# A transformer block on one core: the rounds of its pipeline in a hardware loop, and the input statistics one step later

## What is computed

```python
def _layernorm(x, axis=-1, eps=1e-05):
    m = jnp.mean(x, axis=axis, keepdims=True)
    v = jnp.var(x, axis=axis, keepdims=True)
    return (x - m) / jnp.sqrt(v + eps)

# ffn(x) = x @ int4(kernel) + bias + (x @ a) @ b      128 -> 128, rank 16
x = x + 0.5 * ffn(layernorm(x))
x = x + attn(layernorm(x))     # 16 heads of 64, latent of 32, causal softmax over 512 tokens
x = x + 0.5 * ffn(layernorm(x))

# attn: q = x Wq; latent = x Wkv_down; k = latent Wk_up; v = latent Wv_up
# y = softmax(mask(q k^T / 8)) v; out = y Wout
```

## Time and profile before

| | |
|---|---|
| median of 3 runs | 1116.89 us (1111.92 to 1118.87) |
| the profiled execution | 1111.92 us, its span 1110.2 us |
| mean granted clock of TensorE | 0.959 |
| PE matmul, busy | 995.7 us, 90% of the span, 7518 instructions |
| DVE, busy | 760.2 us, 68%, 2840 instructions |
| ACT, busy | 526.4 us, 47% |
| POOL, busy | 357.0 us, 32% |
| instruction queues | 116 packets, 1.44 MB |

### The profile page before, as it was taken

The page is one execution under the profiler, slowest core; times in us unless marked ns, Lnnn a source line. Parts: engine busy times, 40 slices in busy tenths (PEclk is TensorE's granted clock), DMA queues, the critical chain, the costliest instruction groups (busy, mean ns, idle before and its releaser), DMA issues. The chain is left out here.

```text
span 1110.2 us, 22533 instructions
## 1 busy us (share of the span) xinstructions
PE 995.7 (90%) x7518; PEld 592.3 (53%) x7518; DVE 760.2 (68%) x2840; ACT 526.4 (47%) x1089; POOL 357.0 (32%) x527
## 2 busy tenths in 40 slices
PE   5758899999999999999999999999999999999983
PEld 3434545555555465555555555655555555656453
DVE  2257577778677777778787877777786777776412
ACT  0110445555545545455545555455555455454550
POOL 1010213424243423424243424234242424232432
PEclk9965799999999999999999999999999999999996
DMA  3062323240423324231413333241404233230000
GB/s 73 10 142 58 87 59 96 49 99 21 108 54 68 96 59 106 59 97 25 108 43 77 87 68 96 59 106 43 99 25 105 59 69 87 58 87 2 21 20 10
DMA packets 72436, 74.81 MB, mean 67 GB/s; under 512 B 8880, under 2 KB 46016, under 8 KB 72320
## 3 DMA queue, kind: packets, MB, share of 16 engines
q1 hardware_dynamic: 72320, 73.37, 28.0%
HBM read 9.90 MB, written 8.39 MB: 16 GB/s over the span
## 5 line engine op out<-in xcount | busy, mean ns | idle before, releaser
L750 DVE CUSTOM_DVE_ANT_0 bank<-bank,corner 128x128 f32<-128x128 f32 (+3 forms) x1024 | 487.7, 509 | 223.1 <-PE bank L564 216.4
L405 ACT ACTIVATE probs<-bank 128x512 f32<-128x512 f32 (+1 forms) x704 | 373.9, 558 | 446.5 <-PE bank L517 444.8
L564 PE MATMUL bank<-keys,q_stack 96*128 96x128 f32 (+3 forms) x1024 | 321.6, 362 | 35.8 <-DVE maxima L750 15.9
L371 POOL TENSOR_SCALAR_AFFINE_SELECT probs<-probs 128x512 f32<-128x512 f32 x256 | 162.2, 634 | 573.0 <-ACT probs L405 572.9
L517 PE MATMUL bank<-q_stack,keys 97*128 97x512 f32 (+3 forms) x1024 | 328.2, 380 | 19.7 <-ACT probs L405 19.5
L564 PEld LDWEIGHTS bank<-keys,q_stack 96*128 96x128 f32 x1024 | 188.9, 197 | 166.1 <-issue 99.8
L517 PEld LDWEIGHTS bank<-q_stack,keys 97*128 97x128 f32 x1024 | 172.2, 191 | 109.4 <-ACT probs L405 77.4
L531 PE MATMUL bank<-probs,lat 128*32 128x512 f32 (+3 forms) x2048 | 192.1, 447 | 0.6 <-ACT y_sb L412 0.3
L542 PE MATMUL bank<-probs,group_ones 128*32 128x512 f32 (+3 forms) x2048 | 185.7, 434 | 1.9 <-ACT den L434 0.4
L750 DVE DVE_READ_ACCUMULATOR2_ANT maxima<- 128x1 f32 x1024 | 144.3, 141 | 0.5
L542 PEld LDWEIGHTS bank<-probs,group_ones 128*32 128x32 f32 x2048 | 64.1, 110 | 81.3 <-issue 54.7
(11 more groups left out here) (98 smaller groups left out, 615.4 us busy)
## 6 DMA issues: line engine op xcount, KB each, us to landing
q_stack<-q_high SPq DMA_DIRECT2D x256, 128.0 KB, 2.4
q_stack<-q_low SPq DMA_DIRECT2D x128, 128.0 KB, 2.5
out_dram<-x SPq DMA_DIRECT2D x32, 256.0 KB, 2.3
x_in<-in_L_attn_x_bld_dram SPq DMA_DIRECT2D x16, 256.0 KB, 3.3
x_back<-out_dram SPq DMA_DIRECT2D x16, 256.0 KB, 3.1
keys<-keys_staged SPq DMA_DIRECT2D x16, 192.0 KB, 2.5
lat<-lat_staged SPq DMA_DIRECT2D x16, 64.0 KB, 1.9
wq_in<-in_L_attn_Wq_dram SPq DMA_DIRECT2D x1, 512.0 KB, 5.0
```

Source lines behind the costliest of these rows:

```text
L371: nc.gpsimd.affine_select(out=diag, in_=diag, compare_op=ALU.is_ge, fill=0.0, base=0, pattern=[[0, HG], [1, n]], channel_multiplier=-1).th ...
L405: nc.scalar.activation(probs[s % BUFS][:, e:e + heads, 0:n], scores[u % 2][:, 0:heads * n].rearrange("p (e q) -> p e q", e=heads), ACT.Exp ...
L564: nc.tensor.matmul(bank[:, 0:P * (j + 1)], q_stack[1 - par][0:KS, h, j * P:(j + 1) * P], keys[1 - par][0:KS, 0:P * (j + 1)], start=True, s ...
L750: nc.vector.tensor_tensor_reduce(out=bank, in0=bank, in1=corner[:, L - n:], scale=1.0, scalar=MASKED, op0=ALU.add, op1=ALU.max, accum_out= ...
```

## The change

`rounds` no longer writes out all 19 rounds. Rounds -2 to 1 and 12 to 16 are written out as before. Rounds 2 to 11 become a hardware loop, Fori, of five passes; a pass does an even round t and the odd round t + 1. Inside it t is a register on each engine, and so every wait's value, and the DRAM addresses of the input, of the stored and reloaded x1 and of the output, are computed from it.

The input's preparation is one step or more later, and no longer reaches into the round before: statistics and moments of batch t + 2 on DVE in step 0 of round t, the reciprocal root and right behind it xb on POOL in step 0 ahead of the select, the normalise on DVE in step 1 behind the step's first max unit. ACT copies the second half's maxima in step 1 behind the step's first exponential.

```diff
+        LOOP_FROM, LOOP_TO = 2, B - 4
+
         def rounds(eng, one_round):
-            for t in range(-2, B + 1):
+            for t in range(-2, LOOP_FROM):
+                one_round(t, t % 2)
+            with eng.Fori(LOOP_FROM, LOOP_TO, 2) as t:
+                one_round(t, 0)
+                one_round(t + 1, 1)
+            for t in range(LOOP_TO, B + 1):
                 one_round(t, t % 2)
...
-                def first_rstd(off):
-                    wait_batch_alone(pool, f_moments, t, off, 2, 1)
-                    nc.gpsimd.tensor_scalar(f_var[:, 0], f_mv[:, 0, :, 1], EPS, None, ALU.add).then_inc(f_pool, 1)
-                    wait_batch(pool, f_pool, t, off, 4, 1)
-                    nc.gpsimd.tensor_tensor(f_rstd[:, 0], f_var[:, 0], neg_half[:], ALU.pow).then_inc(f_rstd_made, 1)
-
...
-                    if is_first(t) and s == 0:
-                        first_rstd(2)
-                    if t + 3 < B and s == STEPS - 1:
-                        first_rstd(3)
+                    if prep and s == 0:
+                        wait_batch_alone(pool, f_moments, t, 2, 2, 1)
+                        nc.gpsimd.tensor_scalar(f_var[:, 0], f_mv[:, 0, :, 1], EPS, None, ALU.add).then_inc(f_pool, 1)
+                        wait_batch(pool, f_pool, t, 2, 4, 1)
+                        nc.gpsimd.tensor_tensor(f_rstd[:, 0], f_var[:, 0], neg_half[:], ALU.pow).then_inc(f_rstd_made, 1)
+                        wait_batch(pool, f_free, t, 1, F_UNITS, 2)
+                        nc.gpsimd.tensor_tensor(xb[:], x_in[:, par], half_bias[:, None, :].broadcast_to([P, TT, D]),
+                                                ALU.add).then_inc(xb_made, 1)
...
-                    if prep and s == FRONT_AT[0]:
-                        wait_batch(pool, f_free, t, 1, F_UNITS, 2)
-                        nc.gpsimd.tensor_tensor(xb[:], x_in[:, par], half_bias[:, None, :].broadcast_to([P, TT, D]),
-                                                ALU.add).then_inc(xb_made, 1)
...
+                    if s == 1 and attend:
+                        read_max(1)
...
-                    if s == 0 and attend:
-                        read_max(1)
...
-                    if t + 3 < B and s == STEPS - 2:
-                        wait_batch(dve, x_loaded[1 - par], t, 3, *nth(1 - par))
-                        statistics(x_in[:, 1 - par], f_stats[:, 0], f_dve)
-                        moments(f_stats[:, 0], f_mv[:, 0], f_dve, 2, 1, 3, f_moments)
                     if prep and s == 0 and not is_first(t):
+                        wait_batch(dve, x_loaded[par], t, 2, *nth(par))
+                        statistics(x_in[:, par], f_stats[:, 0], f_dve)
+                        moments(f_stats[:, 0], f_mv[:, 0], f_dve, 2, 1, 2, f_moments)
+                    if prep and s == 1 and not is_first(t):
                         wait_batch(dve, f_rstd_made, t, 2, 2, 1)
                         wait_batch(dve, f_full, t, 1, F_UNITS, 3)
                         for i in range(TT):
```

## The result

The changed kernel takes 1168.36 us (median of 4 runs, 1168.0 to 1170.0) against 1116.64 us: 1.047 times as long, 95% interval 1.044 to 1.051, or 52 us more. The prediction was 1134 us, the right direction at a third of the size; 1168 lies inside its range of 1110 to 1175. Where the time went is not where the prediction had it.

A forecast was written before the change was run, and what follows sets the result against it. The prediction took PE, busy for 90% of the span, as the bound. Its terms, -2 for the reordering, +14 for the jumps and +5 for the waits, gave +17 us and 1134 us, range 1110 to 1175.

The forecast's parts named there:

- The moved statistics: Statistics from step 14 to step 0: 5.5 us gained, 2.8 and 0.8 us lost to a later normalise, -2 us net.
- The jumps: Four jumps back in the loop, each fetching code: 3.5 us each, 14 us in all, bounds 0 and 24 us.
- PE's own part: PE's own jump, partly covered by matmuls already queued: 0.8 us added per jump, between 0 and 3.3.
- The DVE chain: At a jump DVE's statistics start late, so the normalise ends 2.7 us after PE wants it.
- The waits: Wait targets computed from a register in the loop: seven hand-overs a round grow by 67 ns each, 5 us.
- the missing "issue" lines: In the profile before, PE's matmuls in steady rounds never wait for PE's own instruction stream.
- that rival: PE's sequencer becomes the bound through 167 more register instructions a round: 55 us, 1184 us in all; chance 0.20.
- Step 14: PE's two 0.21 us waits, for a freed bank and keys_staged, go in 13 rounds: 5.5 us gained.
- The copy: ACT's 0.25 us copy of the maxima, moved behind step 1's first exponential: zero, or 0.5 us a round if late.
- The select and the queues of POOL and SP: POOL's select behind xb costs about nothing; SP's and POOL's queues have slack at the end of a round.
- the sign of a mis-sized reordering: Unrolled rounds whose length moves by more than 0.5 us would show the reordering was sized wrongly.

The follow-up runs named there:

- order_xb_late: The changed kernel's order with all rounds written out and no loop, but POOL's xb in step 1 behind the select, as before: 1119.51 us, ratio 0.9995.
- order_pe_busy: The changed kernel's order without the loop, plus about 1.6 us of unused matmuls ahead of PE's wait for xn: 1136.02 us.
- loop_only: The order of the kernel before, with rounds 2 to 11 in the loop of five passes: 1150.76 us, ratio 1.026.
- loop_one_pass: The order of the kernel before, rounds 2 to 11 as one pass of a loop that never jumps back, waits computed from a register: 1124.18 us, ratio 1.0056.
- stats_in_gap: The kernel before with DVE's statistics moved from step 14 to step 15 behind the second max unit, POOL's root behind step 15's select: 1110.68 us, ratio 0.994.
- copy_only: The kernel before with only ACT's copy of the second half's maxima moved behind step 1's first exponential: 1117.16 us, ratio 1.000.
- gap_and_max: The kernel before with statistics moved to step 15 and ACT's copy of the first half's maxima ahead of step 11's first exponential: 1092.32 us, ratio 0.978.

## Why the prediction missed the size

**The moved statistics: the step that failed.** The prediction has -2 us for the reordering; it is +39. Its sum had DVE's normalise at 1.12 us wherever it stands, and laid POOL's xb right beside it (366.5 to 367.8) without asking what two engines do to each other. The normalise took 2.78 us. The trace of before had the row for it, in a place that was read for something else, the fill round t = -1, where xb and the normalise meet by chance:

```profile
60.54 1.26 POOL L375 TENSOR_TENSOR xb<-x_in,half_bias 128x512 f32<-128x512 f32 x1
60.60 2.05 DVE L779 TENSOR_SCALAR xn<-x_in,f_mv,f_rstd 128x128 f32<-128x128 f32 x4 [0.87 <-POOL f_rstd L341]
```

Against 1.12 us that is 0.93 us more, as long as xb lasts less the first instruction's own time. order_xb_late shows that this overlap and nothing else in the order costs. The Trainium skill has the rule, "SBUF — State Buffer", section "SBUF: two separate sides": VectorE and GpSimd share a pair of ports by an exclusive lock, VectorE for an instruction in a two-port mode or with two inputs in SBUF, and whoever comes second waits for the whole instruction of the other. The durations agree: the longest single normalise instruction is 1304 ns, about xb's length, and the median 662 ns where a select lies beside. That it is this port, and that the normalise runs in such a mode, no run here shows.

Not every DVE instruction on SBUF is slowed. The reciprocal, from den to den_inv, runs wholly beside the xb of the earlier trace rows in the kernel before and takes the 0.95 us that it takes alone:

```profile
369.45 0.95 DVE L759 RECIPROCAL den_inv<-den 128x128 f32<-128x128 f32 x1 [0.53 <-ACT den L434]
```

**No term for the clock.** The prediction took an idle microsecond of PE for a microsecond. Behind a wait of 1.8 us the granted clock went to 1.2 GHz for 3.4 us, at the waits of a jump for 10 us. order_pe_busy prices it at 21 us or more of the order's 39. The trace of before has a single such stretch in its steady rounds, and its waits there are all under 0.9 us; that a longer one would be paid twice could be asked but not read there.

**The jumps.** 14 us predicted, about 26 measured (loop_only less loop_one_pass). The mechanism is right: DVE waits 2.1 to 2.8 us at a jump where 3.3 was taken, and an announced jump takes half the loop's cost away. The instruction queues say the same. These are the ones of loop_one_pass, with all 19 rounds written out:

```profile
q8 instruction: 63, 1.03, 0.4%
q14 instruction: 70, 0.57, 0.2%
```

That is 133 transfers. loop_only and the changed kernel have the code of 11 rounds and move 130, so the loop's code comes anew in each pass. The path was wrong, and PE's own part was mis-sized: 0.8 us on the ground that matmuls would be queued up; it is 3.5 to 4.4 us a jump in the changed kernel, in two waits. The DVE chain, which the prediction had as the main part (2.7 us), doesn't show, because PE is later than DVE. The rest is again the clock. The Trainium skill's "Runtime: NRT & Kernel Launch", section "Instruction fetch mechanics", says that a taken branch whose target is not in the window held on chip waits for a fetch; the traces agree, with these waits at each of the four jumps. Why there is a second wait no run shows.

**The waits.** 5 us predicted, 6.7 measured, though only 2 us of it show as longer hand-overs. PE's sequencer never became the bound, as the missing "issue" lines said. The range reached 1175 us for that rival alone; that 1168 lies in it is luck.

**Step 14.** 0.42 us a round predicted from two waits, read in one round. The 0.21 us for keys_staged is in all 13 rounds, but the 0.21 us for the freed bank is in two of them only (357.85 and 421.34). The rows carried 3.2 us, not 5.5. stats_in_gap, which frees the same place, nevertheless gains 0.6 us in an undisturbed round, so the size was fair, but not by that reading.

**The copy** was taken at zero and is, by copy_only. The select and the queues of POOL and SP were taken at zero too; no run tests them one by one, but with xb late the whole order costs nothing.

**The signs.** The prediction named an unrolled round that moves by more than 0.5 us as the sign of a mis-sized reordering. Round 1 moved by 2.7.

## To carry to other kernels

When an instruction moves, look at what runs at the same time on DVE and on POOL, and search the whole trace, fill and drain too, for a place where the two already overlap: its duration there is the price. Where TensorE is the bound, a new wait can cost more than its length, as the 1.8 us ones did here, so put slack ahead of it or useful work into it. A body of two such rounds, some 1,860 instructions on PE without its waits, paid at every jump: unroll it, or measure the loop with the jump announced. And split a change that does two things before giving one of them the blame.

## What the runs showed of the hardware

- Filling a wait of PE with matmuls that nobody uses made the kernel 21 us faster; the clock was low for 27 us instead of 71.
- DVE's tensor_scalar from SBUF to SBUF took 1.30 us instead of 0.34 beside POOL's tensor_tensor. DVE's reciprocal beside the same instruction took its usual 0.95 us.
- A jump back costs PE two waits, not one: 2.4 to 2.9 us and, some twenty matmuls later, 0.2 to 2.1 us. With the jump announced 0.7 to 1.0 us stays at each, and a wait of 2.0 us appears behind the loop.
- Some 167 waits of PE and 87 of DVE per round with targets from a register cost 0.4 us in 61.5 us.
- One kernel, same instructions and same waits, had rounds of 61.4 and of 60.0 us by the granted clock (gap_and_max).
